# Embedding look-up and interaction tower: eleven tables by matmul instead of twelve, and gathers that no longer wait for one another

## The chip, the cores and the metric

The kernel runs on one core of one Trainium2 chip. The time is device microseconds of one launch; several runs are made and the median is given. A profile of one execution comes from the hardware profiler.

## What is computed

The batch has 512 samples. Each has 27 ids, one into each of 27 tables with rows of 128 float32 values. One table has 125,000 rows, seven have 12,500 and nineteen have 1,000 or 1,250. Cut to what matters, the reference is:

```
e = stack([tbl_f[ids[:, f]] for f in range(27)], axis=1)      # 512 x 27 x 128
z = einsum('bnd,bmd->bnm', e, e), only the 351 pairs i < j
h = relu(concat([z, dense_ctx], axis=1) @ W_top1 + b_top1)    # 367 -> 512
h = relu(h @ W_top2 + b_top2)                                 # 512 -> 256
y = h @ W_top3                                                # 256 -> 1
```

## The kernel before, in words

**Two ways to fetch a vector.** The batch is cut into 4 tiles of 128 samples. Twelve small tables (`LOOKED_UP_TABLES`, L37) are not gathered: the whole table is loaded to SBUF and the 512 vectors are picked out by matmuls with one-hot matrices. The other 15 tables are gathered from HBM row by row. One indirect DMA on GpSimd (L362) fetches the 128 vectors of one table for one tile, so there are 60 gathers of 64 KB each.

**The look-ups (k = 0 to 11).** A table of 1,000 rows is 8 chunks of 125 rows, one of 1,250 rows is 10 chunks. ScalarE writes the ids, shifted (`idrel`, L623), and the table rounded to fp32r (`hi`, L631). VectorE makes a one-hot matrix for each chunk but the last (L562) and the rest `lo` = table minus `hi` (L566). ScalarE makes the last one-hot (L634, L637). TensorE then does one 512-column matmul for each chunk with `hi` (L401) and one with `lo` (L407). ScalarE copies the result to `embT` (L609). The ids of a later table are spread over the partitions by one matmul (L383). Before all this, VectorE prepares `pick`, with 128 columns for each looked-up table (L547). In the order of the look-ups the tables have 8, 8, 10, 8, 8, 10, 8, 8, 10, 8, 8, 8 chunks; table 9, which the change takes out, is k = 8.

**The gathered vectors** must be transposed on TensorE (L376) before use. They come in groups (t, g) of tile t and group g: four groups of a tile with 4, 4, 4 and 3 tables. `ORDER` (L218) lists the 16 groups. `AT_LOOKUP` (L219) places the first eight of them (tiles 0 and 1) ahead of chosen look-ups, and TensorE does `transposes` and then `look_up(k)` (L490 to L495). The other eight groups stand in `STEPS` (L224 to L236) between the matmuls of the interaction.

**The queue of gathers (L345 to L364).** GpSimd issues the gathers strictly in order of tile and group. Before it issues one, it may wait for several things:
- for tiles after the first, that the same group of the tile before has landed (L349);
- for tile 3, whose buffers are those of tile 0 (`EMB_RING` = 3), that tile 0's group was transposed (L352);
- for the groups with an index over 8, that the group just before has landed (L353 to L356);
- for the gathers from the fifth on, up to group 8, that VectorE has finished a given number of one-hots (L359 to L361).

**After the look-ups** come `gram` (L429, the interaction: per tile 4 units of 8 small matmul groups), copies of the pairs from PSUM to SBUF by VectorE and ScalarE (L522), a move of rows by DMA (L323), and the layers `h1`, `h2` and `y`. The first `gram` needs all looked-up vectors. The transposes of tiles 2 and 3 stand inside the gram phases of tiles 1 and 2. The last of them, of group (3, 3), come just ahead of the last half unit of tile 2's interaction, and the whole of tile 3 follows them.

**The sync queue** loads the tables, three in advance: table k is issued once `lo` of table k-3 is done (L289). Behind the last table it issues W1 and W2, 1.5 MB (L311, L312).

Of the kernel before, what the change touches and what calls it, by code (L numbers as in the profile page):

```python
# [33 lines left out]
P = 128  # L34
QUAD = 32
QUADS = P // QUAD
LOOKED_UP_TABLES = [4, 6, 3, 7, 8, 5, 11, 12, 9, 15, 20, 21]  # L37
PLACES = [f for f in range(27) if f not in LOOKED_UP_TABLES] + LOOKED_UP_TABLES
LOOKED_UP = [*range(27 - len(LOOKED_UP_TABLES), 27)]
ROWS_K = 125  # L40
# [36 lines left out]
def build_tower(nc, ids, ids_looked_up, dense_ctx_t, tables, W1, b1, W2, b2, W3, out):  # L77
# [19 lines left out]
    gathered_features = [f for f in range(FEATS) if f not in LOOKED_UP]  # L97
# [3 lines left out]
    def group(t, g):  # L101

        return FGROUPS[g]

    def rows_gathered(t, g):

        return 16 * sum(len(group(i, g)) for i in range(t + 1))
# [4 lines left out]
    SIZES = sorted(set(CHS))  # L112
    SPRAY = 120
    EMB_RING = 3
    PACED_GROUPS = 8
    RING = 3
    EARLY = 2
    WARM = 5
# [10 lines left out]
    with ExitStack() as ctx:  # L129
# [6 lines left out]
        def sem(name):  # L136
            return ctx.enter_context(nc.semaphore(name))
# [36 lines left out]
        gathered = [sem(f"gathered{g}") for g in range(NFG)]  # L174
# [11 lines left out]
        onehot_by_dve = sem("onehot_by_dve")  # L186
# [29 lines left out]


        ORDER = [(t, g) for t in range(TILES) for g in range(NFG)]  # L218
        AT_LOOKUP = {2: ORDER[0], 4: ORDER[1], 5: ORDER[2], 6: ORDER[3], 8: ORDER[4], 9: ORDER[5], 10: ORDER[6], 11: ORDER[7]}  # L219

        def tr(t, groups):
            return [("transposes", t, g) for g in groups if (t, g) in ORDER[len(AT_LOOKUP):]]

# [7 lines left out]
        t = TILES - 1  # L231
# [28 lines left out]
        def tr_index(t, g):  # L260

            return t * NFG + g
# [71 lines left out]
        @block.gpsimd  # L334
        def _(pool):
            for n, ch in enumerate(SIZES):
                nc.gpsimd.iota(base_i[:, n:n + 1], pattern=[[0, 1]], base=0,
                               channel_multiplier=-ch).then_inc(base_i_ready, 1)
            nc.gpsimd.memset(ident[:, :], 0.0).then_inc(ident_zero, 1)
            pool.wait_ge(ident_zero, 1)  # L340
            nc.gpsimd.affine_select(out=ident[:, :], in_=ident[:, :], compare_op=ALU.not_equal, fill=1.0,
                                    base=0, pattern=[[-1, P]], channel_multiplier=1).then_inc(ident_ready, 1)
            nc.gpsimd.memset(embT[:, 0:TILES // 2, :, FEATS:QUAD], 0.0).then_inc(pads_zeroed, 1)
            pool.wait_ge(ids_loaded, 16)
            for t in range(TILES):  # L345
                for g in range(NFG):

                    if t > 0:
                        pool.wait_ge(gathered[g], rows_gathered(t - 1, g))  # L349
                    if t >= EMB_RING:  # L350

                        pool.wait_ge(transposed, tr_index(t - EMB_RING, g) + 1)  # L352
                    if tr_index(t, g) > PACED_GROUPS:  # L353

                        preceding = ORDER[tr_index(t, g) - 1]
                        pool.wait_ge(gathered[preceding[1]], rows_gathered(*preceding))  # L356
                    for f in group(t, g):
                        n = t * len(gathered_features) + gathered_features.index(f)
                        if n >= 4 and tr_index(t, g) <= PACED_GROUPS:  # L359

                            pool.wait_ge(onehot_by_dve, 27 * n // 10 - 4)  # L361
                        pool.indirect_dma_start(emb[:, t % EMB_RING, gathered_features.index(f), :], None, tables[f],  # L362
                                                bass.IndirectOffsetOnAxis(ids_sb[:, t, f:f + 1], 0),
                                                ).then_inc(gathered[g], 16)  # L364

        @block.tensor
        def _(pe):
            def transposes(t, g):
                n = tr_index(t, g)

                pe.wait_ge(gathered[g], rows_gathered(t, g))
                if n >= 2:
                    pe.wait_ge(embT_by[n % 2], n // 2)
                first = sum(map(len, FGROUPS[:g]))
                for k in range(len(group(t, g))):
                    last = nc.tensor.transpose(tr_ps[:, n % 2, k, :], emb[:, t % EMB_RING, first + k, :], ident[:, :])  # L376
                last.then_inc(transposed, 1)
# [8 lines left out]
            def look_up(k):  # L386
                b = k % 2

                if k >= 2:
                    pe.wait_ge(vectors_out, k - 1)  # L390
                for c in range(CHS[k]):

                    for n, part in enumerate(parts(k)):
                        if c == part.start:
                            pe.wait_ge(hi_ready, parts_to(k) + n + 1)

                    if c < DVE_CHS[k]:
                        pe.wait_ge(onehot_by_dve, sum(DVE_CHS[:k]) + c + 1)
                    else:
                        pe.wait_ge(onehot_by_act, k + 1)  # L400
                    nc.tensor.matmul(acc[:, b, 0:batch], hi[0:ROWS_K, b, c, :], one_hot(k, c),  # L401
                                     start=(c == 0), stop=False)
                for c in range(CHS[k]):
                    for n, part in enumerate(parts(k)):
                        if c == part.start:
                            pe.wait_ge(lo_ready, parts_to(k) + n + 1)
                    last = nc.tensor.matmul(acc[:, b, 0:batch], lo[0:ROWS_K, b, c, :], one_hot(k, c),  # L407
                                            start=False, stop=(c == CHS[k] - 1))
                last.then_inc(looked_up, 1)
# [80 lines left out]
            for k in range(NK):  # L490
                if k in AT_LOOKUP:
                    transposes(*AT_LOOKUP[k])
                look_up(k)
# [40 lines left out]
        def _(dve):  # L534
            def transposes(t, g):
                if tr_index(t, g) % 2 == 0:
                    dve.wait_ge(transposed, tr_index(t, g) + 1)
                    move_vectors(nc.vector.tensor_copy, t, g).then_inc(embT_by[0], 1)
# [16 lines left out]
            for k in range(NK):  # L555
# [8 lines left out]
                for n, c in enumerate(parts(k)):  # L564
                    dve.wait_ge(hi_ready, parts_to(k) + n + 1)
                    nc.vector.tensor_tensor(lo[0:ROWS_K, b, c, :], table[0:ROWS_K, r, c, :], hi[0:ROWS_K, b, c, :],  # L566
                                            ALU.subtract).then_inc(lo_ready, 1)
                if k - 1 in AT_LOOKUP:
                    transposes(*AT_LOOKUP[k - 1])
            if NK - 1 in AT_LOOKUP:  # L570
                transposes(*AT_LOOKUP[NK - 1])
# [139 lines left out]
```

## Time and profile before

| what | value |
|---|---|
| median of 3 runs | 132.7 us (132.5, 132.7, 134.16) |
| the profiled execution | 131.87 us |
| its span, from first to last instruction | 130.0 us |
| around the span | 1.87 us |
| mean granted TensorE clock | 0.972 |
| TensorE busy | 116.0 us (89%) |
| VectorE, ScalarE, GpSimd busy | 87.0, 80.7, 67.8 us |

The page's busy times say how full an engine is, the chain of waits says which work set the end. PE is TensorE (PEld its weight loads), DVE VectorE, ACT ScalarE, POOL GpSimd, SP the sync engine; a q behind a name is that engine's queue. Times in the trace are counted from the start of the span.

### The profile page before, as it was taken

Reading aid. Unit: us, or ns where it says so; the run is one execution under the profiler, and the core shown is the slowest. Engines: PE = TensorE matmul, PEld = TensorE weight load, DVE = VectorE, ACT = ScalarE, POOL = GpSimd, SP = SyncE. Lnnn points to the kernel's source line nnn. Section 1 sums busy time; section 2 is a strip of 40 time slices with the busy share of each in tenths; the row PEclk is TensorE's granted clock in tenths of the full one; section 3 lists DMA queues with packets and bytes.
Section 4 is the critical chain, followed back from the end, with each engine's and each line's share of the span. In section 5 each row is a group of like instructions: output and inputs, shape, how many; then the busy total and the mean of one; then the engine's idle time right before and its main releaser. Section 6 shows DMA issues by size and latency. Waiting matters only on the chain.

```text
span 130.0 us, 2242 instructions
## 1 busy us (share of the span) xinstructions
PE 116.0 (89%) x750; PEld 103.3 (80%) x750; DVE 87.0 (67%) x263; ACT 80.7 (62%) x213; POOL 67.8 (52%) x69
## 2 busy tenths in 40 slices
PE   6499999999999999997999969999996069999992
PEld 6188888888888778885998959999995069899992
DVE  7999899999996999691288881268712005983121
ACT  4488995999789969892388852268630015883220
POOL 7888778668759786845546355547272700000000
PEclk9999999999999999999999999999999757999999
DMA  2899858865974469710201120102120100100000
GB/s 91 225 237 200 194 121 212 206 151 108 218 202 126 122 187 346 234 47 20 59 21 40 42 66 22 47 28 68 27 62 21 40 20 0 24 0 9 9 5 1
DMA packets 5680, 12.54 MB, mean 96 GB/s; under 512 B 2208, under 2 KB 2944, under 8 KB 5541
## 3 DMA queue, kind: packets, MB, share of 16 engines
q1 hardware_dynamic: 3725, 8.44, 24.5%
q0 software_dynamic: 1920, 3.94, 12.7%
q8 instruction: 6, 0.10, 0.3%
q10 hardware_dynamic: 24, 0.02, 0.1%
q14 instruction: 5, 0.04, 0.1%
HBM read 12.15 MB, written 0.00 MB: 93 GB/s over the span
## 4 chain that ended last, share of the span: by engine, by line
PE 52%; DMA 15%; POOL 13%; issue 11%; DVE 3%; ACT 2%; POOLq 1%; DVEq 0%; ACTq 0%
PE acc L401 17%; DMA emb<-in_tbl,ids_sb 15%; PE acc L407 15%; POOL emb L362 13%; PE gram_ps L429 6%; PE tr_ps L376 3%; PE gram_ps L444 3%; PE acc L444 3%; PE gram_ps L383 2%; PE acc L464 1%; PE tr_ps L464 1%; DVE pairs L522 1%; ACT idrel L623 1%; POOLq L129 1%; DVE onehot L562 1%
## 5 line engine op out<-in xcount | busy, mean ns | idle before, releaser
L362 POOL DMA_INDIRECT emb<-in_tbl,ids_sb x60 | 65.6, 1094 | 35.1 <-DMA emb<-in_tbl,ids_sb 13.9
L522 DVE COPY pairs<-gram_ps 26x56 f32<-26x56 f32 (+1 forms) x128 | 26.1, 204 | 16.6 <-PE gram_ps L429 14.8
L562 DVE TENSOR_SCALAR onehot<-idrel 125x512 fp32r<-125x512 f32 x90 | 32.8, 433 | 3.6 <-ACT idrel L623 3.4
L429 PE MATMUL gram_ps<-embT 128*122 128x104 f32 x256 | 31.0, 279 | 1.8 <-ACT embT L609 1.1
L429 PEld LDWEIGHTS gram_ps<-embT 128*122 128x122 f32 x256 | 29.9, 196 | 2.9 <-ACT embT L609 1.5
L522 ACT COPY pairs<-gram_ps 26x56 f32<-26x56 f32 (+1 forms) x128 | 24.9, 195 | 9.0 <-PE gram_ps L429 7.2
L401 PE MATMUL acc<-onehot,hi 125*128 125x512 f32 x102 | 27.9, 419 | 1.0 <-ACT hi L631 1.0
L407 PE MATMUL acc<-onehot,lo 125*128 125x512 f32 x102 | 25.3, 391 | 0.0
L401 PEld LDWEIGHTS acc<-onehot,hi 125*128 125x128 f32 x102 | 19.6, 199 | 5.6 <-ACT hi L631 1.7
L407 PEld LDWEIGHTS acc<-onehot,lo 125*128 125x128 f32 x102 | 19.3, 190 | 4.5 <-DVE lo L566 0.4
L609 ACT COPY embT<-acc 128x512 f32<-128x512 f32 x12 | 13.4, 1115 | 8.0 <-PE acc L407 7.9
L566 DVE TENSOR_TENSOR lo<-table,hi 125x1024 fp32r<-125x1024 f32 (+2 forms) x14 | 15.4, 1114 | 0.0
L376 PE MATMUL tr_ps<-ident,emb 128*128 128x128 f32 x60 | 9.7, 282 | 5.7 <-DMA emb<-in_tbl,ids_sb 5.7
L631 ACT CAST hi<-table 125x1024 fp32r<-125x1024 f32 (+2 forms) x14 | 13.4, 973 | 0.4 <-DMA table<-in_tbl 0.4
L529 ACT COPY embT<-tr_ps 128x512 f32<-128x512 f32 (+1 forms) x8 | 4.5, 565 | 14.6 <-PE tr_ps L376 14.6
L376 PEld LDWEIGHTS tr_ps<-ident,emb 128*128 128x128 f32 x60 | 7.4, 147 | 7.0 <-DMA emb<-in_tbl,ids_sb 6.0
L444 PE MATMUL acc<-pairs,w_sb 128*128 128x128 f32 x96 | 11.8, 278 | 1.3 <-DMA pairs<-pairs 1.3
L444 PEld LDWEIGHTS acc<-pairs,w_sb 128*128 128x128 f32 x96 | 11.1, 192 | 1.6 <-DMA pairs<-pairs 1.6
L623 ACT ACTIVATE idrel<-gram_ps,base_f 125x512 f32<-125x512 f32 x12 | 8.2, 682 | 2.3 <-PE gram_ps L383 2.3
L634 ACT ACTIVATE near<-idrel,chunk 125x512 f32<-125x512 f32 x12 | 8.7, 729 | 0.0
L637 ACT ACTIVATE onehot<-near 125x512 fp32r<-125x512 f32 x12 | 7.6, 634 | 0.4
L529 DVE COPY embT<-tr_ps 128x512 f32<-128x512 f32 x8 | 5.5, 683 | 3.1 <-PE tr_ps L376 3.0
(43 smaller groups left out, 57.1 us busy)
## 6 DMA issues: line engine op xcount, KB each, us to landing
table<-in_tbl SPq DMA_DIRECT2D x8, 480.0 KB
table<-in_tbl SPq DMA_DIRECT2D x3, 600.0 KB
w_sb<-in_W SPq DMA_DIRECT2D x1, 1024.0 KB, 6.6
emb<-in_tbl,ids_sb POOLq DMA_INDIRECT x60, 2.7
w_sb<-in_W SPq DMA_DIRECT2D x1, 512.0 KB, 9.1
table<-in_tbl SPq DMA_DIRECT2D x2, 240.0 KB
pairs<-pairs SPq DMA_DIRECT2D x16, 15.0 KB
table<-in_tbl SPq DMA_DIRECT2D x8, 20.0 KB
```

The costliest lines, as they stand in the source:

```text
L362: pool.indirect_dma_start(emb[:, t % EMB_RING, gathered_features.index(f), :], None, tables[f], bass.IndirectOffsetOnAxis(ids_sb[:, t, f:f ...
L376: last = nc.tensor.transpose(tr_ps[:, n % 2, k, :], emb[:, t % EMB_RING, first + k, :], ident[:, :])
L401: nc.tensor.matmul(acc[:, b, 0:batch], hi[0:ROWS_K, b, c, :], one_hot(k, c), start=(c == 0), stop=False)
L407: last = nc.tensor.matmul(acc[:, b, 0:batch], lo[0:ROWS_K, b, c, :], one_hot(k, c), start=False, stop=(c == CHS[k] - 1))
L429: last = nc.tensor.matmul(gram_ps[0:ROWS, u % 2, g, 0:WIDTH], vectors[:, QUAD * p0:QUAD * p0 + ROWS], embT[:, t, p0:p0 + SG, 1:FEATS], sta ...
L444: last = nc.tensor.matmul(h1_ps(t, n), w1_sb[:, a, P * n:P * (n + 1)], pairs[:, t % 2, a + MOVED_SLOTS, :], start=(a == UNMOVED), stop=(a ...
L522: last = copy(pairs[QUAD * q:QUAD * q + FEATS - 1, t % 2, a:SLOTS, c0:c0 + UNITG], src.rearrange("r g a -> r a g"))
L529: last = copy(embT[:, t, :, f:f + n], tr_ps[:, tr_index(t, g) % 2, k:k + n, :].rearrange("d f p -> d p f"))
L562: nc.vector.tensor_scalar(one_hot(k, c), idrel[0:ROWS_K, b, 0:batch], float(c), None, ALU.is_equal).then_inc(onehot_by_dve, 1)
L566: nc.vector.tensor_tensor(lo[0:ROWS_K, b, c, :], table[0:ROWS_K, r, c, :], hi[0:ROWS_K, b, c, :], ALU.subtract).then_inc(lo_ready, 1)
L609: nc.scalar.copy(embT[:, :, :, LOOKED_UP[k]], acc[:, k % 2, 0:batch].rearrange("d (t p) -> d t p", p=P)).then_inc(vectors_out, 1)
L631: nc.scalar.copy(hi[0:ROWS_K, b, c, :], table[0:ROWS_K, r, c, :]).then_inc(hi_ready, 1)
```

## The change

Table 9 leaves the list of looked-up tables and becomes the sixteenth gathered one. So there are 11 look-ups, 64 gathers in place of 60, and every group has 4 tables. The look-ups after k = 7 move up by one: the new k = 8, 9, 10 are the old k = 9, 10, 11. Two of the waits ahead of a gather go: that on the group just before, and that on VectorE's one-hots. The waits on the same group of the tile before, and on the buffer of tile 0, stay. The first eight groups of transposes are placed ahead of look-ups 2, 3, 4, 5, 6, 8, 9, 10 instead of 2, 4, 5, 6, 8, 9, 10, 11.

```diff
-LOOKED_UP_TABLES = [4, 6, 3, 7, 8, 5, 11, 12, 9, 15, 20, 21]
+LOOKED_UP_TABLES = [4, 6, 3, 7, 8, 5, 11, 12, 15, 20, 21]
...
-    PACED_GROUPS = 8
...
-        AT_LOOKUP = {2: ORDER[0], 4: ORDER[1], 5: ORDER[2], 6: ORDER[3], 8: ORDER[4], 9: ORDER[5], 10: ORDER[6], 11: ORDER[7]}
+        AT_LOOKUP = {2: ORDER[0], 3: ORDER[1], 4: ORDER[2], 5: ORDER[3], 6: ORDER[4], 8: ORDER[5], 9: ORDER[6], 10: ORDER[7]}
...
                         pool.wait_ge(transposed, tr_index(t - EMB_RING, g) + 1)
-                    if tr_index(t, g) > PACED_GROUPS:
-
-                        preceding = ORDER[tr_index(t, g) - 1]
-                        pool.wait_ge(gathered[preceding[1]], rows_gathered(*preceding))
                     for f in group(t, g):
-                        n = t * len(gathered_features) + gathered_features.index(f)
-                        if n >= 4 and tr_index(t, g) <= PACED_GROUPS:
-
-                            pool.wait_ge(onehot_by_dve, 27 * n // 10 - 4)
                         pool.indirect_dma_start(emb[:, t % EMB_RING, gathered_features.index(f), :], None, tables[f],
```

## Rows read from the trace of the kernel before

**Rows 1.** The page: the span, and the chain's shares of it by engine

```profile
span 130.0 us, 2242 instructions
...
PE 52%; DMA 15%; POOL 13%; issue 11%; DVE 3%; ACT 2%; POOLq 1%; DVEq 0%; ACTq 0%
```

**Rows 2.** The chain that ended last, 89 to 95 us: start, duration, what

```profile
89.79 2.56 DMA emb<-in_tbl,ids_sb
...
92.41 0.72 issue
93.13 0.94 POOL emb L362
94.07 0.30 issue
```

**Rows 3.** TensorE in order of time: start, us, work, idle time before

```profile
34.72 0.49 PE L376 MATMUL tr_ps<-ident,emb 128*128 128x128 f32 x3
...
43.19 2.55 PE L401 MATMUL acc<-onehot,hi 125*128 125x512 f32 x10
...
48.33 0.60 PE L376 MATMUL tr_ps<-ident,emb 128*128 128x128 f32 x4
...
52.66 0.60 PE L376 MATMUL tr_ps<-ident,emb 128*128 128x128 f32 x4
...
62.00 7.48 PE L429 MATMUL gram_ps<-embT 128*122 128x104 f32 x64 [1.10 <-ACT embT L609]
...
99.50 0.66 PE L376 MATMUL tr_ps<-ident,emb 128*128 128x128 f32 x4 [0.98 <-DMA emb<-in_tbl,ids_sb]
...
105.25 0.90 PE L376 MATMUL tr_ps<-ident,emb 128*128 128x128 f32 x3 [4.75 <-DMA emb<-in_tbl,ids_sb]
105.95 5.93 PE L429 MATMUL gram_ps<-embT 128*122 128x104 f32 x40
```

**Rows 4.** Stretches: length, busy us (instructions) of PE, PEld, DVE, ACT, POOL, clock, DMA

```profile
105.20:109.00 3.80, 3.75 (x18) 3.75 (x19) 1.12 (x6) 1.61 (x7) 0.00 (x0) 0.50 0.00 0
84.70:88.70 4.00, 3.89 (x37) 3.72 (x36) 2.91 (x15) 3.16 (x15) 2.04 (x3) 1.00 0.08 21
```

**Rows 5.** Who waited for whom: us in total, times, longest

```profile
POOL emb L362 <- issue: 9.6, 32, 0.3
POOL emb L362 <- DVE onehot L562: 9.1, 21, 1.1
```

**Rows 6.** GpSimd in order of time: gathers 20, 28, 32, 34 and 60

```profile
32.80 0.94 POOL L362 DMA_INDIRECT emb<-in_tbl,ids_sb  x1 [0.51 <-DVE onehot L562]
...
45.36 1.10 POOL L362 DMA_INDIRECT emb<-in_tbl,ids_sb  x1 [0.30 <-issue]
...
52.46 1.89 POOL L362 DMA_INDIRECT emb<-in_tbl,ids_sb  x1 [0.30 <-DVE onehot L562]
...
55.98 1.06 POOL L362 DMA_INDIRECT emb<-in_tbl,ids_sb  x1 [0.30 <-DVE onehot L562]
...
102.74 0.94 POOL L362 DMA_INDIRECT emb<-in_tbl,ids_sb  x1 [0.30 <-issue]
```

**Rows 7.** VectorE in order of time: the cast of pick, and one subtraction

```profile
1.67 2.14 DVE L547 CAST pick<-ident 128x1536 fp32r<-128x1536 f32 x1
...
52.32 1.21 DVE L566 TENSOR_TENSOR lo<-table,hi 125x1024 fp32r<-125x1024 f32 x1
```

**Rows 8.** Line 362: landing of gathers issued in 57:105, 16:28, 46:52

```profile
DMA to landing us min/median/max: 2.4/2.5/3.5
...
DMA to landing us min/median/max: 2.7/3.7/5.8
...
DMA to landing us min/median/max: 5.1/6.9/7.3
```

**Rows 9.** The sync queue in order of time: the issue of W1

```profile
46.38 0.35 SPq L311 DMA_DIRECT2D w_sb<-in_W  x1
```

## The prediction

> **What bounds the kernel now.** The page comes first: TensorE is busy for 89% of the span, so one would call it the bound. The chain says otherwise, since only 52% of it is TensorE and 13% + 15% is GpSimd and the gathers' DMA [rows 1]. So I read the chain in order of time. From 56 us to 105 us it holds gathers alone, in a pattern of one round per group: three or four gathers of 0.94 us with 0.30 us of issue between them, then the landing of the last, 2.56 us from its start, then 0.72 us until the next group begins [rows 2]. A group of four thus takes 3 x 1.24 + 2.56 + 0.05 + 0.72 = about 7.1 us where four gathers alone would take 5.0.
>
> TensorE in order of time shows what this costs. In the gram phase it falls behind the gathers only at the end: it stands 0.98 us before group (3, 2) and 4.75 us before (3, 3) [rows 3], 5.73 us together. Everything of tile 3 comes after that. The wait has a second price. In the 3.8 us behind it the granted clock is 0.50 (1.2 of 2.4 GHz) and 18 matmuls get done; at clock 1.00, between 84.7 and 88.7, 37 of them take 4.0 us [rows 4]. So the work of 18/37 x 4.0 = 1.95 us took 3.8 us, 1.85 us lost; I use 1.8.
>
> Before 61 us TensorE hardly ever stands: look-ups follow each other, and the one longer gap after them is 1.10 us for ScalarE's last copy [rows 3]. So there are two bounds in a row, TensorE with the look-ups and then the gathers, and the change touches both.
>
> **The change part by part**, against the profiled span of 130.0 us.
>
> (1) *Table 9 is not looked up.* Its hi matmuls begin at 43.19 and the next step, the transposes ahead of the following look-up, at 48.33 [rows 3]: **-5.14 us** on TensorE, which ends the look-ups. ScalarE and VectorE lose their share of that table too. Its loading goes as well.
>
> (2) *pick is narrower.* Its cast took 2.14 us for 12 tables [rows 7] and stands ahead of the first matmul: 2.14/12 = 0.18 at most, 0 if the first table's landing takes its place. I take **-0.15**.
>
> (3) *Four more transposes.* Four take 0.60 us, three 0.49 [rows 3], so 0.11 each: **+0.44**, two in the look-ups, one in tile 2 and one in tile 3. Their copies are one column block wider, beside TensorE's work: nothing.
>
> (4) *No wait on the preceding group.* In the gram phase gathers then follow each other at 0.94 + 0.30 = 1.24 us, which is the rate inside a group already [rows 2]. The 34th gather starts at 55.98 now [rows 6]; the last of 64 would start 30 x 1.24 = 37.2 us later, at 93.2, and land 2.5 us on [rows 8], at 95.7. If the other removed wait brings its most, see (5), it is 92.9. TensorE, without its two waits, would want group (3, 3) at 105.25 - 5.73 = 99.52, less 5.14 and 0.15, plus 3 x 0.11, and plus the stalls of (6), here called s: 94.6 + s. With s = 2 that is 96.6 and all gathers are there. So both waits go, **-5.73**, and the slow stretch behind them, **-1.8**. With s = 0 and late gathers 1.1 us of wait would come back, too short to count on a slow clock (the 1.10 us gap at 62.00 was not followed by one). What stays is the same-group wait one tile back, 12 gathers or more earlier, and the ring, whose tile 0 is transposed by about 30 us while tile 3's first gather would come about 70 us: both at nothing.
>
> (5) *No wait on one-hots.* 21 gathers were held by VectorE, for 9.1 us, which is 0.43 each; those held by nothing took 9.6/32 = 0.30 for issue [rows 5]. So at most 21 x 0.13 = 2.8 us come forward by the 34th gather. Less is likely. From the 20th to the 34th a gather came every (55.98 - 32.80)/14 = 1.66 us [rows 6], far above 1.24, and a good part is no wait. VectorE's subtraction runs from 52.32 to 53.53 [rows 7]; the gather that begins at 52.46 lasts 1.89 us and ends at 54.35 [rows 6], 0.82 behind it. One that begins with no subtraction about needs 0.94. GpSimd is shut out until a subtraction ends, and a gather released earlier may run into it. I count 1 to 2.8 us.
>
> The Trainium skill says otherwise of such an instruction: its page "SBUF — State Buffer", section "Who interferes with whom", has a two-input VectorE operation take only the read interface of the port pair shared with GpSimd, while descriptor generation needs the write side (it marks this as inferred). The trace disagrees by the 0.95 us above. What the rule would make of the time stands with the rivals.
>
> (6) *Transposes placed one look-up earlier.* This is where a new stall can come: TensorE does everything in order, so a group that has not landed stops the look-up behind it. I compare when TensorE gets there, without stalls, with when the last gather of the group lands.
> - Group (1, 0), gathers 17 to 20, is wanted ahead of look-up 6, where (0, 3) stood at 34.72 [rows 3]: 34.72 - 0.15 + 0.44 (four transposes that now stand earlier, by the table's order) = 35.0. Gather 20 starts at 32.80 [rows 6] less up to 1 us, and lands 2.7 to 5.8 us later, middle 3.7 [rows 8]: 35.5 to 36.5 in the middle. Stall about 0.5 to 1.5.
> - Group (1, 2), gathers 25 to 28, is wanted ahead of look-up 9, where the old look-up 10 had it at 52.66 [rows 3]: less 5.14 and 0.15, plus 0.22, gives 47.6. Gather 28 starts at 45.36 [rows 6] less up to 2, and landing takes longer here. W1 and W2 (1.5 MB) were issued at 46.38 [rows 9] and the gathers issued around it took 5.1 to 7.3 us to land [rows 8]. They now go out behind the load of the last table, which waits for the subtraction of look-up 7 and no longer for that of 8, so some 5 us sooner, at 41 to 42, right before these gathers. 43.4 to 45.4 plus 5.1 gives 48.5 to 50.5: stall 1 to 3. The longest case of the rows, 7.3 us, would give 5.
> - Groups (0, 2), (0, 3) and (1, 1) come out within half a us of their time by the same reckoning, and (1, 3), gather 32, starts at 52.46 less up to 2.8 and lands after W has passed, about when it is wanted at 51.7.
> These do not add up: a stall moves TensorE back and the next group is in time by as much. The largest counts. I take **+2.0**, with 0 to 5 as the ends, 2.0 because it is the middle of the nearest case, (1, 2).
>
> Sum: 130.0 - 5.14 - 0.15 + 0.44 - 5.73 - 1.8 + 2.0 = 119.6 us of span. With 1.87 around it, 121.5. The profiled execution of 131.87 is 0.8 below the median of the three runs, 132.7; I add about half of that and predict **121.8 us**.
>
> **The rivals.**
>
> *A, the forecast*: TensorE is the bound throughout and stalls about 2 us in the look-ups, 120.3 to 123.5 for stalls from 0.5 to 3.5.
>
> *B, no stall in the look-ups.* Gathers that no longer wait run ahead far enough. Then s = 0: 117.6 + 1.87 = 119.5, up to 1.1 more if the last group is late, so about 120.0. For it: the removed waits of 2.8 us. Against it: the subtractions, and W's load, which moves onto just these gathers. By the skill's rule above, B would be the case: no gather would be held by a subtraction, and the 0.95 us of each such hold would come off. Since the row shows the hold, the rule adds little to B's chance.
>
> *C, the collision with W is as bad as its worst rows.* Gathers land 7.3 us late, TensorE stands for 5 us in one piece, and as behind the 4.75 us wait of now its clock falls. Price 5.0 + 1.8: the span is 119.6 - 2.0 + 6.8 = 124.4, time 126.3. For it: the 6.9 us middle of those rows. Against it: an earlier stall in look-up 6 would take some of it off, and the gathers are up to 2 us sooner.
>
> *D, slower.* VectorE's and ScalarE's copies of pairs hold GpSimd, now that gathers run without pause beside them, as the look-ups' work does. Then each of the last 30 gathers takes 1.66 us, the last starts at 55.98 + 49.8 = 105.8 and lands at 108.3, 3.1 us after the 105.2 of now: 131.87 + 3.1 + 0.2 = 135.2. It decides from 1.56 us per gather on, when the last landing is no sooner than now, and is slower by 2% from about 1.65. Against it: gathers beside such copies take 0.94 us now, as at 93.13 [rows 2] with copies running before and after.
>
> *E, the change does not do what it says.* One of the waits that stay takes the place of those removed, and only the table's 5 us and no gather time is won; since the end is set by the gathers, almost nothing moves: 131 to 134. By (4) no such wait is near.
>
> **How the numbers follow.** A 0.60, B 0.21, C 0.13, D 0.03, E 0.03. The time is A's. The range goes from below B, 119.0, where its 119.5 holds and (2) and (3) come out at their ends, to 125.5, past A's upper end and into C, as far as its stall is 5 us but the clock recovers early. That leaves out the rest of C and D and E, 0.15 or so. About 2% is what a measurement of this kernel can tell from no change; A, B and C are all faster by more: 0.94. Within 2%: E and a part of D, 0.04. Slower: 0.02.
>
> **What would show it.** Right: the chain from 56 us on is TensorE; no idle time before the transposes of (3, 2) and (3, 3), clock 1.00 to the end; gathers of 0.94 us every 1.24 us, the last starting at 90 to 93 us; the first gram at 58 to 60 us; a stall before the transposes ahead of look-up 6 or 9 that names a gather. Wrong: first gram at 56.9 or before (B); idle of over 3.5 us in the look-ups and a clock under 1.00 behind it (C); gathers in the gram phase over 1.3 us apart (D); a wait other than issue before gathers (E). I would be most wrong about the landing times near W's load, which the trace shows only once, with another spacing of gathers.

## The result, and the profile after

The changed kernel takes 121.98 us in the median of four runs (121.58 to 123.11), the kernel before 132.6. The ratio is 0.9193, with a 95% interval of 0.9097 to 0.9289: faster, by 8%. Some executions of a kernel take over 1.5% longer than its fastest one; the ratios of this document leave those out, the medians do not. The prediction was 121.8 us. The profiled execution took 122.14 us for a span of 120.3.

The page: the span, the granted clock over the span, and the chain's shares by engine.

```profile
span 120.3 us, 2184 instructions
...
PEclk9999999999999999999999999999999999999999
...
PE 42%; POOL 28%; DMA 11%; issue 8%; DVE 5%; SPq 4%; ACT 1%; POOLq 0%
```

Two things differ from before ([rows 1], and a mean clock of 0.972): the clock stays at 9 or more everywhere, and the 15% of the gathers' DMA in the chain are gone (5% of gather DMA are left, by the lines of that view). The 28% of GpSimd are a new bound, but a short-lived one. They belong to the first 43 us, where the chain runs back through the gathers to the 28th, whose landing at 49.36 releases the transposes of group (1, 2). TensorE stands only 0.34 us for that one, and 1.89 us for gathers in all, so it is nearly a bound itself; but up to 49.4 us a faster TensorE alone would have gained nothing.

TensorE in order of time (start, us, work, idle time before and what ended it):

```profile
3.76 1.19 PE L374 MATMUL gram_ps<-id_rows_r,pick 128*128 128x512 f32 x2 [0.20 <-DVE id_rows_r L541]
...
28.87 0.39 PE L374 MATMUL gram_ps<-id_rows_r,pick 128*128 128x512 f32 x1
30.82 0.66 PE L367 MATMUL tr_ps<-ident,emb 128*128 128x128 f32 x4 [1.55 <-DMA emb<-in_tbl,ids_sb]
...
35.86 0.39 PE L374 MATMUL gram_ps<-id_rows_r,pick 128*128 128x512 f32 x1
36.31 0.66 PE L367 MATMUL tr_ps<-ident,emb 128*128 128x128 f32 x4
...
48.67 0.39 PE L374 MATMUL gram_ps<-id_rows_r,pick 128*128 128x512 f32 x1
49.40 0.66 PE L367 MATMUL tr_ps<-ident,emb 128*128 128x128 f32 x4 [0.34 <-DMA emb<-in_tbl,ids_sb]
...
58.91 7.47 PE L420 MATMUL gram_ps<-embT 128*122 128x104 f32 x64 [1.10 <-ACT embT L600]
...
74.18 3.62 PE L435 MATMUL acc<-pairs,w_sb 128*128 128x128 f32 x30 [1.53 <-DMA pairs<-pairs]
...
89.81 3.62 PE L435 MATMUL acc<-pairs,w_sb 128*128 128x128 f32 x30 [0.59 <-DMA pairs<-pairs]
...
97.12 0.63 PE L367 MATMUL tr_ps<-ident,emb 128*128 128x128 f32 x4
97.59 8.54 PE L420 MATMUL gram_ps<-embT 128*122 128x104 f32 x72
```

To be read against [rows 3]. The first gram starts at 58.91, and was at 62.00. The transposes of (3, 3) stand at 97.12 and wait for nothing, where 105.25 had 4.75 us of idle time before it, and the 72 matmuls behind them take 8.54 us at full clock. In the look-ups there is a new 1.55 us before group (0, 3), at 30.82, and 0.34 before (1, 2), at 49.40. Where nothing is waited for, transposes start 0.24 us after the start of the spread matmul ahead of them (the L374 lines). So the losses at 30.82, 36.31 and 49.40 are 1.7, 0.2 and 0.5: 2.4 us together.

GpSimd in order of time: gathers 1, 16, 28, 34 and the last, the 64th.

```profile
3.14 1.11 POOL L353 DMA_INDIRECT emb<-in_tbl,ids_sb  x1
...
25.28 1.17 POOL L353 DMA_INDIRECT emb<-in_tbl,ids_sb  x1 [0.30 <-issue]
...
42.92 1.08 POOL L353 DMA_INDIRECT emb<-in_tbl,ids_sb  x1 [0.30 <-issue]
...
51.21 1.03 POOL L353 DMA_INDIRECT emb<-in_tbl,ids_sb  x1 [0.30 <-issue]
...
89.47 0.94 POOL L353 DMA_INDIRECT emb<-in_tbl,ids_sb  x1 [0.31 <-issue]
```

Before, gather 34 started at 55.98 and gather 60 at 102.74 [rows 6]; now they are 1.25 us apart from 57 us on, the last starts at 89.47, and none waits for anything but issue:

```profile
POOL emb L353 <- issue: 19.2, 63, 0.3
```

That is 63 of the 64, 0.30 us each. Gone are the waits on VectorE of [rows 5], and the wait on the preceding group, which the same view of the kernel before has as

```profile
POOL emb L362 <- DMA emb<-in_tbl,ids_sb: 13.9, 6, 2.4
```

with a seventh of 2.4 us that it puts down to TensorE.

### The profile page after: what moved, and what is told of

Read it like the earlier page. It is cut to its first block, busy times and chain, and to the rows that moved or that the text cites. A ratio compares the mean times of both kernels' runs of the same rounds, so it can differ in the third digit from the quotient of the medians.

```text
span 120.3 us, 2184 instructions
## 1 busy us (share of the span) xinstructions
PE 110.2 (92%) x733; PEld 97.7 (81%) x733; DVE 81.5 (68%) x253; ACT 76.9 (64%) x208; POOL 70.3 (58%) x73
## 4 chain that ended last, share of the span: by engine, by line
PE 42%; POOL 28%; DMA 11%; issue 8%; DVE 5%; SPq 4%; ACT 1%; POOLq 0%
POOL emb L353 26%; PE gram_ps L420 14%; PE acc L435 9%; DMA emb<-in_tbl,ids_sb 5%; DMA pairs<-pairs 5%; PE acc L455 5%; DVE pairs L513 4%; SPq L322 4%; PE tr_ps L367 3%; PE gram_ps L435 3%; PE acc L392 3%; PE acc L398 3%; PE tr_ps L455 1%; POOL embT L342 1%; ACT embT L600 1%
## 5 line engine op out<-in xcount | busy, mean ns | idle before, releaser
L353 POOL DMA_INDIRECT emb<-in_tbl,ids_sb x64 | 68.1, 1064 | 19.3 <-issue 19.2
L553 DVE TENSOR_SCALAR onehot<-idrel 125x512 fp32r<-125x512 f32 x81 | 29.3, 430 | 5.3 <-ACT idrel L614 5.2
L392 PE MATMUL acc<-onehot,hi 125*128 125x512 f32 x92 | 25.0, 417 | 1.0 <-ACT hi L622 1.0
L398 PE MATMUL acc<-onehot,lo 125*128 125x512 f32 x92 | 22.8, 390 | 0.0
L392 PEld LDWEIGHTS acc<-onehot,hi 125*128 125x128 f32 x92 | 17.7, 199 | 5.1 <-ACT hi L622 1.7
L398 PEld LDWEIGHTS acc<-onehot,lo 125*128 125x128 f32 x92 | 17.2, 188 | 3.8 <-DVE lo L557 0.2
L600 ACT COPY embT<-acc 128x512 f32<-128x512 f32 x11 | 12.0, 1093 | 8.8 <-PE acc L398 8.8
L557 DVE TENSOR_TENSOR lo<-table,hi 125x1024 fp32r<-125x1024 f32 (+2 forms) x13 | 14.0, 1088 | 0.0
L520 ACT COPY embT<-tr_ps 128x512 f32<-128x512 f32 x8 | 4.9, 618 | 8.3 <-PE tr_ps L367 8.3
L579 DVE TENSOR_SCALAR h1T<-acc,b_sb 128x128 f32<-128x128 f32 x6 | 1.8, 347 | 7.9 <-PE acc L435 7.9
```

The source lines that it names most:

```text
L553: nc.vector.tensor_scalar(one_hot(k, c), idrel[0:ROWS_K, b, 0:batch], float(c), None, ALU.is_equal).then_inc(onehot_by_dve, 1)
L600: nc.scalar.copy(embT[:, :, :, LOOKED_UP[k]], acc[:, k % 2, 0:batch].rearrange("d (t p) -> d t p", p=P)).then_inc(vectors_out, 1)
```

## The experiments

Each run is held against the kernel before on the same chip. Theory throughout: the wait on the preceding group held the last gathers and with them TensorE's clock; table 9 is worth its TensorE time; and the earlier transposes cost about 2 us of stalls.

### The wait on the preceding group, removed alone

The kernel before, with twelve look-ups, without this:

```diff
-                    if tr_index(t, g) > PACED_GROUPS:
-
-                        preceding = ORDER[tr_index(t, g) - 1]
-                        pool.wait_ge(gathered[preceding[1]], rows_gathered(*preceding))
```

> Theory (round trips): the wait on the preceding group alone makes the 5.73 us of idle TensorE and the 1.8 us of slow clock behind it. Without it, with twelve look-ups and all else as before, the first gram still starts at 62.0, gathers from the 35th on start every 1.25 us, group (3,3) has landed by about 92, TensorE does not stand there: span 130.0 - 5.73 - 1.8 = 122.5, time 124.3. Moves of pairs land about 0.3 and 0.7 us later beside denser gathers, so up to 125.2. Rival (the gathers as a whole are too slow, the wait only hides that): the last gather still lands behind TensorE and the time stays over 129.

Measured: 124.32 us, ratio 0.9301 (0.9211 to 0.9391). TensorE, in order of time:

```profile
62.72 7.48 PE L425 MATMUL gram_ps<-embT 128*122 128x104 f32 x64 [1.10 <-ACT embT L605]
...
100.16 0.53 PE L372 MATMUL tr_ps<-ident,emb 128*128 128x128 f32 x3
100.52 8.53 PE L425 MATMUL gram_ps<-embT 128*122 128x104 f32 x72
```

The first gram starts 0.7 us later than in the profile of the kernel before, and that arises in the very first look-up, which is over at 12.71 instead of 11.88. (In eight undisturbed profiles of kernels with eleven look-ups it is over at any time from 10.45 to 12.53.) The transposes of (3, 3) stand at 100.16 with no idle time before them, and the mean clock is 1.0. This one wait was worth 8.3 of the 10.6 us by the medians, 9.3 by the ratio. The rival falls.

### The same wait, put back into the changed kernel

```diff
+                    if tr_index(t, g) > 8:
+
+                        preceding = ORDER[tr_index(t, g) - 1]
+                        pool.wait_ge(gathered[preceding[1]], rows_gathered(*preceding))
```

> Theory (round trips): with the wait put back, groups 9 to 15 go in rounds of 7.0 us from 56.5 on, the last lands at about 105.3, TensorE stands 5 us or more before (3,3) and its clock falls: span about 130, time 131.5 to 133, nothing left of the gain though table 9 is gone. The waits on moved pairs fall back to 1.3 and 0. Rival (fewer look-ups and the placement carry the gain): 124 or less.

Measured: 134.61 us, ratio 1.0156 (1.0103 to 1.0208): nothing is left of the gain, and it may be a little slower than the kernel before, though by less than 2%. TensorE:

```profile
102.08 0.66 PE L371 MATMUL tr_ps<-ident,emb 128*128 128x128 f32 x4 [3.79 <-DMA emb<-in_tbl,ids_sb]
...
109.13 1.12 PE L371 MATMUL tr_ps<-ident,emb 128*128 128x128 f32 x4 [5.86 <-DMA emb<-in_tbl,ids_sb]
```

Direction right, size 2 to 3 us short. I had let the rounds begin at 56.5; they begin at 59.48, behind group 8, and seven groups of 7.1 us on average then end with a landing at 109.1. With four gathers in every round (before, two of the last eight rounds had three) the gathers take longer than in the kernel before, and the table's 5 us on TensorE are worth nothing. Fewer look-ups pay only with the wait gone.

### The wait on one-hots, put back

```diff
                     for f in group(t, g):
+                        n = t * len(gathered_features) + gathered_features.index(f)
+                        if n >= 4 and tr_index(t, g) <= 8:
+
+                            pool.wait_ge(onehot_by_dve, 24 * n // 10 - 4)
```

> The wait on one-hots put back with one gather every 2.4 one-hots (the old 2.7 does not fit 81 one-hots). Theory: gathers of the look-up phase start up to 2 us later, the stall before (0,3), 1.7 us now, grows to 2 to 2.7, those at look-ups 6 and 9 too: 0.5 to 1.5 us more, 122.5 to 123.6. Rival (GpSimd is held by subtractions anyway, so that wait costs nothing): within 0.3 us of 122.0.

Measured: 122.82 us in the median of four runs that spread from 120.35 to 124.25, and no ratio was formed from them. Inconclusive in time. In the trace the stall before (0, 3) is 1.57 us, as without the wait, and that before (1, 2) is 1.64 instead of 0.34; the first gram starts at 61.12 instead of 58.91. In both traces it hangs on gather 28, the last of (1, 2): here it starts at 44.02 and lands 7.56 us later, there at 42.92 and 6.44 us later, and that makes the 2.2 us. Half of it is the later start. Whether the slower landing comes of the wait is not shown, and TensorE would have been some of it late anyway, since its first look-up ended at 12.09 here and at 11.00 there.

### Transposes placed later, inside the look-ups

```diff
-        AT_LOOKUP = {2: ORDER[0], 3: ORDER[1], 4: ORDER[2], 5: ORDER[3], 6: ORDER[4], 8: ORDER[5], 9: ORDER[6], 10: ORDER[7]}
+        AT_LOOKUP = {2: ORDER[0], 4: ORDER[1], 5: ORDER[2], 6: ORDER[3], 7: ORDER[4], 8: ORDER[5], 9: ORDER[6], 10: ORDER[7]}
```

> Transposes ahead of look-ups 2,4,5,6,7,8,9,10. Theory 1 (the stalls do not add, the largest counts, and W's load makes (1,2) late whatever stands before): no stall before (0,3), but TensorE reaches look-up 9 some 1.9 us sooner, gather 28 lands at 49.4 as now, so it stands 2 us there: 121.5 to 122.5, no gain. Theory 2 (the stall comes from placing (0,3) early): 1.7 us less, about 120.3.

Measured: 122.19 us (four runs, 120.19 to 123.26), against 121.98 of the changed kernel, which did not run beside it; no ratio was formed, and the time says only that no large gain is there. TensorE:

```profile
43.84 0.66 PE L367 MATMUL tr_ps<-ident,emb 128*128 128x128 f32 x4 [1.52 <-DMA emb<-in_tbl,ids_sb]
...
49.41 0.66 PE L367 MATMUL tr_ps<-ident,emb 128*128 128x128 f32 x4 [1.03 <-DMA emb<-in_tbl,ids_sb]
...
58.91 7.47 PE L420 MATMUL gram_ps<-embT 128*122 128x104 f32 x64 [1.10 <-ACT embT L600]
```

(0, 3) is no longer waited for, but (1, 1) at 43.84 and (1, 2) at 49.41 now are, 2.55 us together, and the first gram starts at 58.91, where it was. That it is the same to the hundredth is chance. Gather 28 starts 1.8 us later than in the changed kernel and lands 1.8 us faster:

```profile
44.73 4.63 DMA emb<-in_tbl,ids_sb
```

But the pattern is the expected one. Stalls of this kind don't add up. A stall that is avoided early is paid later, as long as some group is wanted before it lands. Theory 1 holds; I had named one group for the 2 us where it was two.

### Two groups moved behind the last look-up

```diff
-        AT_LOOKUP = {2: ORDER[0], 3: ORDER[1], 4: ORDER[2], 5: ORDER[3], 6: ORDER[4], 8: ORDER[5], 9: ORDER[6], 10: ORDER[7]}
+        AT_LOOKUP = {2: ORDER[0], 4: ORDER[1], 5: ORDER[2], 6: ORDER[3], 8: ORDER[4], 9: ORDER[5]}
```

This kernel ran twice. The first time:

> Transposes ahead of look-ups 2,4,5,6,8,9, and (1,2), (1,3) behind the last look-up, where TensorE stands 1.10 us for ScalarE's copy. Theory (all of the stalls come from groups wanted before they land): every group is wanted 2 us or more after it lands, no stall is left in the look-ups (2.4 us less) and 0.7 us of transposes fill the gap: 3 us less, span 117.3, time 119 to 119.5. Last gathers land at 92, TensorE wants them at about 94. Rival (other waits, on one-hots or on ScalarE, take the place): 121 or more.

It took 164.61 us (156.21 to 174.57), on one chip and at one time with three others that all took about 155 us or more; the last section of the experiments is about that. The second time, beside the changed kernel on the same chip:

> The same kernel as after_gap: (1,2) and (1,3) transposed behind the last look-up, the rest ahead of look-ups 2,4,5,6,8,9. In the disturbed run its first gram started at 56.2 where the changed kernel has 58.9 and 59.4, with no stall before. On an undisturbed chip 61.4 us follow, as in the changed kernel: span 117.6, time 119.4, some 2.5 us under after_third beside it. On a chip that delays TensorE's signals: over 150 for both.

> The changed kernel, unedited, on the same chip as gap_again. Undisturbed: 121 to 122.5, with 2 to 3 us of TensorE stalls before transposes in the look-ups. Theory C (the delay of TensorE's signals belongs to a chip and to free-running gathers): if this is the chip of after_gap, over 150; theory K (it came from the edits): 122 there too.

Measured: gap_again 117.95 us, ratio to the kernel before 0.8872 (0.8807 to 0.8936); after_third 120.75, ratio 0.9098 (0.9041 to 0.9154). The intervals don't touch: the placement gives another 2.8 us by the medians, where 2.5 were expected, and beats both kernels. TensorE in gap_again:

```profile
56.89 7.47 PE L420 MATMUL gram_ps<-embT 128*122 128x104 f32 x64 [0.24 <-ACT embT L600]
```

and in after_third:

```profile
30.55 0.66 PE L367 MATMUL tr_ps<-ident,emb 128*128 128x128 f32 x4 [1.18 <-DMA emb<-in_tbl,ids_sb]
...
36.26 0.66 PE L367 MATMUL tr_ps<-ident,emb 128*128 128x128 f32 x4 [0.27 <-DMA emb<-in_tbl,ids_sb]
...
49.21 0.66 PE L367 MATMUL tr_ps<-ident,emb 128*128 128x128 f32 x4 [0.20 <-DMA emb<-in_tbl,ids_sb]
...
58.71 7.48 PE L420 MATMUL gram_ps<-embT 128*122 128x104 f32 x64 [1.10 <-ACT embT L600]
```

The stalls before transposes are gone, and the two groups fill the 1.10 us in which TensorE waits for ScalarE's copy; 0.24 us of it are left. The first gram comes 1.8 us sooner although the first look-up of this profile ended 1.3 us later (12.53 against 11.19), so from there on the placement is worth 3.1 us.

### W1 and W2 loaded later

```diff
+            sp.wait_ge(lo_ready, parts_to(NK))
             sp.dma_start(w1_sb[:, :, :], W1.rearrange("p (a n) -> p a n", a=K_SLOTS)).then_inc(w1_loaded, 16)
```

> W1 and W2 are issued after the last subtraction, at about 54.7, placement as in the changed kernel. Theory 1 (W's load delays gathers 27 to 31): gathers issued 42 to 48 land in 2.7 to 4 us instead of up to 6.4, the stall of 0.5 us at look-up 9 goes, that of 1.7 at (0,3) stays: 0.4 us less, 121.5. W lands by 64, well before h1 at 72. Theory 2 (W does not matter): landing of those gathers stays at 5 us or more.

Measured: 156.48 us (154.91 to 161.91), among the disturbed runs. Up to 50 us the trace is clean, and it decides little. The stall before (0, 3) is there, 1.51 us, so W has no part in it. None stands before (1, 2), but TensorE came there only at 50.15, after the 49.36 at which gather 28 had landed in the changed kernel; here that gather started at 43.87. How much of the second stall is W's load stays open. In the changed kernel's chain that gather is this line (start, us from issue to landing):

```profile
42.92 6.44 DMA emb<-in_tbl,ids_sb
```

W's load was issued at 42.54 there. Gathers in the quiet part take 2.5 us [rows 8]. But long landings do not need W: gather 16 of the changed kernel, which started at 25.28, held TensorE until 30.82, so it took 5.5 us with only the loads of tables beside it.

### Subtractions cut into pieces

```diff
-                    nc.vector.tensor_tensor(lo[0:ROWS_K, b, c, :], table[0:ROWS_K, r, c, :], hi[0:ROWS_K, b, c, :],
-                                            ALU.subtract).then_inc(lo_ready, 1)
+                    for c0 in range(c.start, c.stop, 2):
+                        c2 = slice(c0, c0 + 2)
+                        last = nc.vector.tensor_tensor(lo[0:ROWS_K, b, c2, :], table[0:ROWS_K, r, c2, :],
+                                                       hi[0:ROWS_K, b, c2, :], ALU.subtract)
+                    last.then_inc(lo_ready, 1)
```

> Each subtraction is cut into 4 or 5 pieces of 2 chunks (about 0.35 us each), with the same bytes. Theory (GpSimd is held until the subtraction at work ends): no gather over 1.5 us in the look-ups; those of 1.89 us are gone, the 34th gather starts 1 us or so earlier than 51.2. VectorE works 0.2 us longer per look-up, TensorE may wait for lo, so the time is 121.5 to 122.5. Rival (GpSimd is held for as long as VectorE works at subtractions at all, a whole series): gathers of 1.9 us or more remain.

Measured: 177.6 us (171.91 to 177.83), among the disturbed runs, so its time says nothing. The first 22 us are clean. VectorE's four pieces, in one line, and the gathers beside them:

```profile
20.43 1.42 DVE L559 TENSOR_TENSOR lo<-table,hi 125x256 fp32r<-125x256 f32 x4
```

```profile
19.57 1.09 POOL L353 DMA_INDIRECT emb<-in_tbl,ids_sb  x1 [0.30 <-issue]
20.96 1.04 POOL L353 DMA_INDIRECT emb<-in_tbl,ids_sb  x1 [0.30 <-issue]
```

The gather that starts at 20.96, amid the pieces, takes 1.04 us. With one whole subtraction from 20.12 to 21.33 the changed kernel's gather at 20.26 takes 1.89. So a gather waits for the piece at work, not for the series, as the theory has it. In time it was not settled what that is worth.

The trace of the changed kernel says more exactly what is held. One subtraction and the two gathers that overlap it:

```profile
34.49 1.21 DVE L557 TENSOR_TENSOR lo<-table,hi 125x1024 fp32r<-125x1024 f32 x1
```

```profile
33.96 1.09 POOL L353 DMA_INDIRECT emb<-in_tbl,ids_sb  x1 [0.30 <-issue]
35.36 1.17 POOL L353 DMA_INDIRECT emb<-in_tbl,ids_sb  x1 [0.31 <-issue]
```

The first starts before the subtraction and ends in the middle of it, held by nothing: 1.09 us is what a gather takes beside one-hots. The second starts inside it and ends 0.83 us behind its end. So it is throughout that trace from 15 us on: of nine gathers that start inside a subtraction, eight end 0.81 to 0.83 us behind it (the ninth starts in its last hundredth), and seven that had started before one end inside it after 1.08 to 1.09 us. A subtraction holds only the start of a gather.

### pick made 12 blocks wide again

```diff
-        pick = sb("pick", [P, NK, P], F32R)
+        pick = sb("pick", [P, NK + 1, P], F32R)
...
-            nc.vector.tensor_copy(pick[:, :, :], ident[:, 0:NK].unsqueeze(2).broadcast_to([P, NK, P])).then_inc(pick_ready, 1)
+            nc.vector.tensor_copy(pick[:, :, :], ident[:, 0:NK + 1].unsqueeze(2).broadcast_to([P, NK + 1, P])).then_inc(pick_ready, 1)
```

> pick is made 12 blocks wide again, of which 11 are used. Theory (an even number of blocks lets the cast run at twice the rate, but through ports it shares with GpSimd, so that it waits for GpSimd's memset to end at 2.99; an odd number runs at the single rate at once): the cast takes 2.14 us again instead of 1.62, the first matmul starts at 4.28 instead of 3.76, 0.5 us more in all. Rival (the cast's time goes with its width): 1.62 x 12/11 = 1.77, 0.15 us more.

Measured: 167.2 us (155.02 to 173.7), among the disturbed runs; its first microseconds are clean. VectorE with 12 blocks:

```profile
1.67 2.12 DVE L538 CAST pick<-ident 128x1536 fp32r<-128x1536 f32 x1
```

and with 11, in the changed kernel:

```profile
1.67 1.62 DVE L538 CAST pick<-ident 128x1408 fp32r<-128x1408 f32 x1
```

2.12 against 1.62 us, and the first matmul starts at 4.26 against 3.76. One block less is worth 0.5 us, and the rival, that the time goes with the width, falls: it had 1.77 us for 12 blocks. That the odd number is what counts is the theory, and only 11 and 12 were run.

### The disturbed runs, and what was tried against them

The four kernels after_gap, after_late_w, after_wide_pick and after_split_lo ran on one chip and took 155 to 178 us there, while the kernel before, run beside them, took 131.81. In the profile of after_gap all is as planned until 58 us. Then TensorE:

```profile
56.23 3.66 PE L420 MATMUL gram_ps<-embT 128*122 128x104 f32 x32 [0.25 <-ACT embT L600]
70.61 3.62 PE L420 MATMUL gram_ps<-embT 128*122 128x104 f32 x16 [10.72 <-issue]
98.68 7.40 PE L420 MATMUL gram_ps<-embT 128*122 128x104 f32 x48 [24.44 <-DVE pairs L513]
```

and VectorE, which copies out what these matmuls make:

```profile
68.82 1.72 DVE L513 COPY pairs<-gram_ps 26x48 f32<-26x48 f32 x8 [12.08 <-remote]
96.89 3.48 DVE L513 COPY pairs<-gram_ps 26x48 f32<-26x48 f32 x16 [26.34 <-remote]
```

TensorE has issued the first two units by 59.9 us. VectorE, and ScalarE with it, gets to see the first at 68.82 and the second at 96.89, and sits idle for 12 and 26 us. GpSimd meanwhile issues gathers as evenly as ever, and the last of them starts at 90.32:

```profile
90.32 0.94 POOL L353 DMA_INDIRECT emb<-in_tbl,ids_sb  x1 [0.30 <-issue]
```

Four us after it has landed all is normal again and stays so. In after_wide_pick the same sets in during a look-up, and there one sees that TensorE itself issues slowly, though it waits for no other engine:

```profile
65.08 0.59 PE L398 MATMUL acc<-onehot,lo 125*128 125x512 f32 x1 [1.39 <-issue]
67.18 0.59 PE L398 MATMUL acc<-onehot,lo 125*128 125x512 f32 x1 [1.51 <-issue]
68.58 0.59 PE L398 MATMUL acc<-onehot,lo 125*128 125x512 f32 x1 [0.81 <-issue]
```

One matmul in 1.4 to 2.1 us, where 0.23 is usual. In the other two it begins at about 50 us (after_late_w, where ScalarE's copy at 52.84 comes 2.7 us behind TensorE's work) and at 23 us (after_split_lo).

One of these traces has a pause of the gathers in it. In after_split_lo GpSimd stands from 74.77 to 83.21 us:

```profile
83.21 0.94 POOL L353 DMA_INDIRECT emb<-in_tbl,ids_sb  x1 [8.44 <-remote]
```

TensorE's last slow matmul starts at 79.52, inside that pause. From 83.97 on it works without such gaps, though GpSimd issues eight more gathers beside it. So here, once, TensorE recovered when the gathers paused and before they were over.

Two kernels were then run on another chip:

> The changed kernel itself, unedited. In the call before, four kernels with free-running gathers took 155 to 178 us on one chip, where the kernel before took its usual 132; TensorE's signals came 10 to 36 us late while gathers ran. Theory C (it is a matter of the chip, and of gathers without a pause): on such a chip the changed kernel itself takes over 150 us, on any other about 122. Theory K (it is a matter of the four edits): 122 on any chip.

Measured: 121.16 us, ratio 0.9123 (0.906 to 0.9187).

```diff
-        return 16 * sum(len(group(i, g)) for i in range(t + 1))
+        return 16 * 3 * (t + 1)
...
+        gathered_last = [sem(f"gathered_last{g}") for g in range(NFG)]
...
-        AT_LOOKUP = {2: ORDER[0], 3: ORDER[1], 4: ORDER[2], 5: ORDER[3], 6: ORDER[4], 8: ORDER[5], 9: ORDER[6], 10: ORDER[7]}
+        AT_LOOKUP = {2: ORDER[0], 4: ORDER[1], 5: ORDER[2], 6: ORDER[3], 8: ORDER[4], 9: ORDER[5]}
...
-                        pool.wait_ge(gathered[g], rows_gathered(t - 1, g))
+                        pool.wait_ge(gathered_last[g], 16 * t)
+                    if tr_index(t, g) > 8:
+
+                        pt, pg = ORDER[tr_index(t, g) - 1]
+                        pool.wait_ge(gathered[pg], rows_gathered(pt, pg))
...
+                        n = t * len(gathered_features) + gathered_features.index(f)
+                        if n >= 4 and tr_index(t, g) <= 8:
+
+                            pool.wait_ge(onehot_by_dve, 24 * n // 10 - 4)
...
-                                                ).then_inc(gathered[g], 16)
+                                                ).then_inc((gathered_last if f == group(t, g)[3] else gathered)[g], 16)
```

> Eleven look-ups, transposes placed as in after_gap, gathers paced: by one-hots up to group 8 and, from group 9 on, each group waits until the third gather of the group before has landed, which leaves about 0.7 us of pause in a round of 5.7 us. On a chip without the disturbance: last gather starts at about 96 and lands at 98, 4 us behind TensorE, so 122 to 125. On a chip with it, if pauses are the cure: the same 122 to 125; if the pauses must be longer: over 140.

Measured: 125.69 us, ratio 0.9496 (0.9432 to 0.956); the last gather starts at 96.08 and TensorE stands 4.82 us for its group:

```profile
98.70 1.09 PE L377 MATMUL tr_ps<-ident,emb 128*128 128x128 f32 x4 [4.82 <-issue]
```

That is the price of the softer wait where nothing is disturbed, and no run shows that it would help where something is. The disturbance did not come back. Two other chips ran free gathers without it: one ran after_again, the other the first four experiments and the pair gap_again and after_third. The kernel after_gap, at 164.61 us in the disturbed runs, ran at 117.95 us as gap_again, so that edit alone does not bring it, and theory K falls for it; the other three edits ran nowhere else. What is shown is that free-running gathers and that chip came together with it in four kernels out of four, and that the paced kernel before ran there undisturbed. Whether it belongs to the chip, or to that quarter of an hour, is open, and so is whether the unedited changed kernel would show it: it never ran there.

## Why the prediction was right

The time was right within 0.2 us, and so was the mechanism. That it came so close is in part luck. The span was 0.7 us longer than the sum (120.3 against 119.6): pick gave 0.4 more than reckoned, the stalls took 0.4 more, and a term of 0.9 was missing. Against that I had put the median 0.3 us above the profiled execution, and it came 0.2 below it.

(1) *Table 9, -5.14.* Fits, as what is left of a sum; no run takes the table out alone. From the start of look-up 1 to the first gram it was 12.12 to 62.00 before, and is 11.23 to 58.91: 2.2 us less, which is 5.14 less 2.4 of stalls, less some 0.5 of transposes and trifles.

(2) *pick, -0.15.* Mis-sized: 0.52. The first matmul starts at 3.76 and was at 4.28. I had scaled by width; after_wide_pick shows that going from 12 blocks to 11 gives the 0.5 us.

(3) *Four more transposes, +0.44.* Held as far as can be read: a group of four takes 0.60 to 0.66 us, where three took 0.49 to 0.53.

(4) *-5.73 and -1.8.* Held, and shown twice: by before_no_group_wait (124.32, with 124.3 expected) and by after_group_wait. The last gather came even sooner than reckoned, 89.47 against 93.2 at its start, or 90.4 with all of (5), so rival D and the 1.1 us of a late (3, 3) never came near. Gathers beside the copies of pairs took 0.94 us throughout.

(5) *Gathers of the look-up phase 1 to 2.8 us sooner.* Too low: gather 34 starts at 51.21 instead of 55.98, 4.8 us. The removed wait gave its most, 2.8 us. The other 2.0 are gathers that take less: the first one 1.11 us instead of 1.64, and up to gather 33 seven instead of eight that a subtraction holds, for less time. My fear that freed gathers would run into subtractions more often did not come true. And "GpSimd is shut out until a subtraction ends" is too wide: only gathers that start inside one are held (after_split_lo above). This goes against the sentence of the Trainium skill that I quoted, but I had read too little of that section ("SBUF — State Buffer", "Who interferes with whom"). It also says that a VectorE operation with two SBUF inputs contends with a GpSimd instruction that reads SBUF, and a gather takes its ids from there; with that the trace agrees, by the 0.95 us of the longest hold.

(6) *+2.0 of stalls.* Right in size, 2.4, and right in the group that sets it. Without its first two stalls TensorE would have wanted (1, 2) at 47.0, and that group landed at 49.36: 2.4 late, where I had 1 to 3 and took 2.0. What was wrong is where TensorE stands. I had "Groups (0, 2), (0, 3) and (1, 1) come out within half a us of their time", and (0, 3) took 1.7 of the 2.4. Its last gather started at 25.28, and the transposes that wait for it began at 30.82: 5.5 us to land, and I had taken the middle 3.7 of [rows 8] where the range went to 5.8. It cost nothing in the end, since the stall before (1, 2) was then 0.5 us in place of 2.4. That only the largest counts, on which the single figure rested, is what after_later bears out.

One term was missing. TensorE's wait for the moved pairs, 1.26 us before, is 1.53 now, and tile 1 has a new one of 0.59 (74.18 and 89.81 above). These are DMAs on the same 16 engines as the gathers, which are denser now. But after_third, with the same gathers, has 1.08 and no second wait, so I don't call the gathers its cause. It makes 0.9 us of this one profile and explains why its gram phase shortened by 6.6 us (68.0 to 61.4) and not by 7.3.

The rivals: B (no stall, 119.5 to 120.0) is what the other placement made real, at 117.95, with the filled gap on top. C did not come: gather 28 took 6.44 us and not 7.3, the longest stall was 1.55 us, and the clock stayed at full speed. E fell with the first experiment. A slower case did occur, on one chip, and it was not among the rivals.

## What to carry to other kernels

Where a queue waits for the landing of what it has just issued, the round trip is paid in every round: here 2.1 us in 7.1, hidden until TensorE caught up with it. Such a wait is worth nothing for order if the buffers are guarded otherwise; but before it goes, find out on more than one chip what it may have been there for.

When in-order work is placed among other work, the sum of the stalls is set by the group that is latest against its need. Moving others back inside the same stretch gave nothing here; moving the late ones into a gap that exists anyway gave 2.8 us.

## What the hardware showed that I had not expected

**Eleven blocks are cast faster than twelve.** The cast that makes pick takes 1.62 us for 11 blocks of 128 (1408 values) and 2.12 to 2.14 for 12 (1536). GpSimd writes a memset beside it:

```profile
1.58 1.41 POOL L342 MEMSET embT<- 128x1280 f32 x1
```

With 12 blocks the cast ends some 0.8 us after the end of the memset at 2.99, which would be 1536 values at nearly 2 per ns; with 11 it ends at 3.29, 1408 values in 1.6 us, about 0.9 per ns, right through the memset. The first gather behind it is shorter too, 1.11 us against 1.64. The Trainium skill offers an explanation, which no run here tests: "VectorE: DVE Perf Modes", section "Mode 2×_2P — use both read ports for one tensor", has a double rate that uses both ports where the outermost dimensions are even, and "SBUF — State Buffer", section "Who interferes with whom", has that mode shut out by a GpSimd instruction at work. The trace agrees with that by the 0.5 us that the first matmul moves. But the first of these sections allows the double rate for an odd outermost dimension too, if it is equal in source and destination, and the profile does not show how the two were laid out. So why 11 blocks ran at the single rate is not settled.

**A subtraction holds the start of a gather and nothing else of it.** A gather that starts inside a two-input subtraction on VectorE ends 0.81 to 0.83 us behind it in the changed kernel's trace, and with a subtraction of 1.21 us up to 0.95 us late; one that started as little as 0.19 us before the subtraction is not held at all.

**On one chip TensorE was held up while GpSimd gathered without pause**: its signals came 10 to 36 us late, its matmuls one in 1.4 to 2.8 us, from some point after 22 us until the gathers were over or, in one trace, had paused for 8 us, and the kernels took 155 to 178 us. One of them took 118 us elsewhere. The kernel before, with pauses between gathers, ran on that chip as on the others; but it differs in more than the pauses, and no kernel with pauses added ran there. The mechanism stays open.
